# The routed blocks' early chains one unit sooner in the last step of a Mamba scan

## The chip, the cores and the metric

The program runs on one core of a Trainium2 chip. The metric is the device time in microseconds (us) of the whole program. Its engines each work through their own instructions in order and wait on semaphores: TensorE (PE: matrix products), VectorE (DVE), ScalarE (ACT), GpSimd (POOL), and SyncE (SP), which here only issues transfers.

## The reference

One transformer-like layer, float32, for 2 sequences of 2048 tokens with 256 features:

```python
h = _layernorm(x) * (1 + ca) + sa                      # modulated by a condition
x = x + ga * mixer(h)                                  # layernorm, then a Mamba forward and one backward in time
h = _layernorm(x) * (1 + cb) + sb
x = x + gb * ffn(h)

# in each Mamba (512 channels, 16 states), per time step:
h = h * exp(dt_t * A) + (dt_t * u_t) * B_t;  y = sum_n h * C_t
# out: (y + xc * D) * silu(z) @ W_out.T

# ffn: the best 2 of 8 experts by softmax of h @ gate_w.T, and a shared part for every token:
z = silu(xt @ sw1.T) * (xt @ sw2.T) @ sw3.T
```

## The kernel before

**Tiling.** The 4096 tokens are 8 blocks of 512. The mixer runs in 16 steps `q` (a block forward, a block backward, and so on). A step has 16 units `t`, each 32 channels by 16 states laid out as 128 partitions x 4 groups x 512 times; so there are 256 units `T = 16 q + t`. Four units are a chunk (128 channels).

**One unit.** ScalarE writes the four groups' decays `exp(dt * A)` into PSUM (`decay`, L1399, two at `n == 0` and two at `n == 2`), and at groups that start from a kept state adds it to the first input (`seed`, L1431). TensorE spreads a unit's 32 channels over the partitions (`spread_input`, L2480) into the one bank `PS_U`; VectorE multiplies it by B (`multiply`, L1914). For units 3, 7, 10, 12 and 15 of a step GpSimd does that multiply (L1046) from a copy that SyncE brings, except for unit 7 of the last step (`SPARED`). VectorE runs two scans (`scan`, L1935). GpSimd multiplies the result by C (`weigh`, L1058). When a chunk is complete TensorE sums it (`sum_chunk`, L2491 and L2495), and VectorE gates it (`gate_y`, L1900). `multiply(T + 1)` on VectorE stands ahead of `scan(T, 0)`, and waits for the `spread_input(T + 1)` that belongs to it.

**Order.** Nothing is scheduled by a program: each engine's order is the order in which its loop over `T` (on ScalarE: over `T` and `n` = 0 to 3) issues, and tables such as `Z_AT = [(5, 2), ...]` say at which `(t, n)` ScalarE does a side job. Within one `T`, TensorE's loop issues `spread_input`, then `sum_chunk`, and at its end `early_blocks(t)`. Two PSUM banks are shared in turn by everything that isn't scan work (`bank_uses`, `take_bank`, `filled`, `drained`): a product into a bank waits until the bank's last content has been copied out, which is ScalarE's work nearly always. The order of these uses is one list, and it is the same before and after.

**The last step (q = 15, units 240 to 255).** Two blocks of the feed-forward part are begun while the last scans run ("early blocks", p = 0 and 1): GpSimd adds the mixer's result (`weigh_mixed`, `add_mixed`); VectorE takes statistics (`norm_statistics`, L1970 and L1973); ScalarE copies them (`variance`); GpSimd takes the power (`norm_power`, L1105, `scale_mean`); ScalarE normalises (`normalise_tokens`, L1541); TensorE turns the block (`turn_early`, L2504), ScalarE copies it (`copy_turned_early`, L1524); TensorE makes the router's logits (`router_early`, L2515) and the shared part's products of block 0, four "g" (gate) and four "u", and four "g" of block 1 (`hidden_early`, L2535), each copied by ScalarE (`copy_g0`, `copy_u0`, `copy_g1`). In the same step ScalarE copies four z chunks (L1314) and takes silu of them at (7, 3), with a table load ahead of it and one behind. When the scans are over, VectorE, TensorE, ScalarE and GpSimd go through the eight blocks' feed-forward and routing by hand-written orders (from 1666 us on), and then through the tiles of the experts.

Of the kernel before, what the change touches and what calls it, by code (L numbers as in the profile page):

```python
# [29 lines left out]
STEPS = 2 * NBLK  # L30
# [42 lines left out]
OUT_AT = [(4, 1), (5, 0)]  # L73
Z_AT = [(5, 2), (6, 1), (6, 3), (7, 1)]

FIRST_Z_AT = [(5, 0), (5, 2), (6, 0), (6, 1)]
SILU_Z_AT = (7, 3)
XDBL_AT = (8, 0)
# [2 lines left out]
COPY_DT_AT = [(11, 1), (12, 2), (13, 3), (15, 2)]  # L81
XP0_AT, XP1_AT, CONV0_AT = (11, 3), (12, 3), (14, 1)

G0_AT = [(9, 3), (10, 1), (10, 3), (11, 1)]
U0_AT = [(12, 0), (12, 2), (12, 3), (12, 3)]
G1_AT = [(14, 1), (15, 1)]

EXP_AND_LN = "natural_log_exp_and_others"

# [113 lines left out]
def mixer_and_experts(nc, A, out):  # L203
    with ExitStack() as top:
# [760 lines left out]
        def _(pool):  # L965
# [153 lines left out]
            for T in range(ALL_UNITS):  # L1119
                q, t = divmod(T, UNITS)  # L1120
                ahead = q + 1 < STEPS
                if T + 2 < ALL_UNITS and on_pool(T + 2):
                    multiply(T + 2)
                if q == STEPS - 1 and t == 7:
                    add_mixed(1)
                if 0 < T < ALL_UNITS - 1:
                    weigh(T - 1)
                if t == 12 and ahead:
                    step_input(q + 1, 0)
                if T == 2:  # L1130
                    step_input(q, 2)
                if t == (6 if q > 0 else 9):
                    step_input(q, 3)
                if t == 14 and ahead:
                    step_input(q + 1, 1)
                if q == STEPS - 1:
                    if t == 2:
                        weigh_mixed(0)
                    if t == 3:
                        add_mixed(0)  # L1140
                        nc.gpsimd.memset(minus_half3[:], -0.5).then_inc(f_const, 1)
                    if t == 5:
                        pool.wait_ge(f_const, 1)
                        norm_power(0)
                        scale_mean(0)
                        weigh_mixed(1)
                    if t == 8:
                        norm_power(1)
                        scale_mean(1)
            def scatter(p, k):  # L1150
# [44 lines left out]
        def _(act):  # L1195
# [331 lines left out]
            def variance(p):  # L1527

                act.wait_ge(a_step, 2 * NT * (p + 1))
                nc.scalar.activation(fvar[:, p], fmv[:, p, :, 1], ACT.Copy, bias=EPS).then_inc(f_var, 1)  # L1530
                nc.scalar.activation(fmv[:, p, :, 0], fmv[:, p, :, 0], ACT.Copy, scale=-1.0).then_inc(f_var, 1)
# [67 lines left out]

            def early_blocks(t, n):  # L1600

                if (t, n) == (6, 0):
                    variance(0)
                if (t, n) == (6, 3):
                    normalise_tokens(0)
                if (t, n) in ((8, 0), (8, 1)):
                    copy_turned_early(0, n)
                if (t, n) == (9, 0):
                    copy_router(0)
                if (t, n) == (9, 2):  # L1610
                    variance(1)
                if (t, n) == (10, 3):
                    normalise_tokens(1)
                for c in range(NC):
                    if (t, n) == G0_AT[c]:
                        copy_g0(c)
                    if (t, n) == U0_AT[c]:
                        copy_u0(c)
                if (t, n) == (12, 1):
                    exp_scores(0)  # L1620
                if (t, n) == (13, 1):
                    copy_turned_early(1, 0)
                    copy_turned_early(1, 1)
                if (t, n) == (13, 3):
                    copy_router(1)
                if (t, n) in G1_AT:
                    copy_g1(G1_AT.index((t, n)))

            for T in range(ALL_UNITS):
                q, t = divmod(T, UNITS)  # L1630
                ahead = q + 1 < STEPS
                for n in range(NG):
# [27 lines left out]
                            back_to_exp()  # L1660
                    if q > 0 and (t, n) in OUT_AT:
                        copy_out(q - 1, OUT_AT.index((t, n)))
                    if (t, n) in (Z_AT if q > 0 else FIRST_Z_AT):
                        copy_z(q, (Z_AT if q > 0 else FIRST_Z_AT).index((t, n)))
                    if (t, n) == (XDBL_AT if q > 0 else FIRST_XDBL_AT) and ahead:
                        copy_x_dbl(q + 1)
                    if (T, n) == (6, 3):
# [188 lines left out]
        def _(dve):  # L1856
# [259 lines left out]

            def early_blocks(t):

                if t == 5:
                    norm_statistics(0)  # L2120
                if t == 8:
                    norm_statistics(1)
                if t == 11:
                    shift_logits(0)

            for D in range(2):
# [231 lines left out]
        def _(pe):  # L2358
# [179 lines left out]

            def early_blocks(t):

                if t == 7:
                    turn_early(0, 0)
                    turn_early(0, 1)
                if t == 8:
                    pe.wait_ge(f_gate_loaded, 48)
                    router_early(0)
                    pe.wait_ge(f_sw_loaded, 32)
                    hidden_early("g", 0, sw1, 0)
                    hidden_early("g", 0, sw1, 1)
                if t == 10:  # L2550
                    hidden_early("g", 0, sw1, 2)
                    turn_logits0()
                if t == 11:
                    hidden_early("g", 0, sw1, 3)
                    for c in range(NC):
                        hidden_early("u", 0, sw2, c)
                if t == 12:
                    turn_early(1, 0)
                    turn_early(1, 1)
                    router_early(1)  # L2560
                    hidden_early("g", 1, sw1, 0)
                if t == 14:
                    for c in range(1, NC):
                        hidden_early("g", 1, sw1, c)
                    turn_logits1()

            turn_block(0)
# [29 lines left out]
            for T in range(ALL_UNITS):  # L2597
# [27 lines left out]
                if T == 5:  # L2625
                    project_dt(0, 3)
                if T == SPARED - 2:
                    spread_input(T + 2)
                    project_z(q, 1)
                    project_z(q, 2)  # L2630
                if t % GN == 1 and T > GN:
                    sum_chunk(T // GN - 1)
# [391 lines left out]
```

## Time and profile before

| | us |
|---|---|
| three runs | 2057.31, 2058.60, 2059.46 |
| their median | 2058.6 |
| the profiled execution's own time | 2058.04 |
| its span | 2056.2 |
| busy: VectorE, TensorE, GpSimd, ScalarE | 1925.5, 1813.9, 1798.3, 1599.3 |
| units 240 to 255 on VectorE | about 1558 to 1665.7 |

A busy share over the whole program mixes three stages: the scans (to 1665.7 us), the blocks' feed-forward and routing (to about 1837 us), and the experts' tiles (to the end). The change touches only the last step of the first stage, so what counts is which engine has no idle time there and who waits for whom at the passage to the second stage.

### The profile page before, as it was taken

To read this page: it belongs to the slowest core of one execution; us is meant where nothing else is said; L and a number is where in the kernel's file an instruction comes from. 1 tells how busy PE (TensorE), PEld (TensorE's weight loads), DVE (VectorE), ACT (ScalarE), POOL (GpSimd) and SP (SyncE) were. 2 spreads that over 40 slices of the span, in tenths; PEclk is the share of its full clock that TensorE was granted. 3 is DMA by queue.
4 is the path that set the end of the run, shared out by engine and by line. 5 is a ranking of instruction groups with operands and counts; after the bars stand their busy time and mean duration, and the time that the engine had idled before them with its cause. 6 is when DMAs were issued, how large, how long until landed. Compare 5 with 4: busy or idle time off the path is not lost.

```text
span 2056.2 us, 25386 instructions
## 1 busy us (share of the span) xinstructions
PE 1813.9 (88%) x6768; PEld 829.7 (40%) x6768; DVE 1925.5 (94%) x1820; ACT 1599.3 (78%) x3362; POOL 1798.3 (87%) x612
## 2 busy tenths in 40 slices
PE   7788898979898979788898889898977799999997
PEld 3333333424242423232323233332322256569996
DVE  7999999999999999999999999999999998857776
ACT  5886779898989898877788898989896844546664
POOL 5689999999999999999999999999999953545555
PEclk9999898989898989898989989898987899999999
DMA  7736454544545353535362635354545334635555
GB/s 268 244 117 152 105 138 110 134 108 121 124 116 125 109 133 105 124 106 143 85 164 72 157 92 141 100 131 115 131 97 146 112 126 140 253 135 91 94 94 76
DMA packets 140653, 263.93 MB, mean 128 GB/s; under 512 B 21840, under 2 KB 44368, under 8 KB 139488
## 3 DMA queue, kind: packets, MB, share of 16 engines
q1 hardware_dynamic: 125920, 240.58, 43.3%
q0 software_dynamic: 13296, 17.80, 5.0%
q10 hardware_dynamic: 1296, 3.93, 0.5%
q8 instruction: 56, 0.92, 0.2%
q14 instruction: 85, 0.70, 0.1%
HBM read 193.10 MB, written 70.19 MB: 128 GB/s over the span
## 4 chain that ended last, share of the span: by engine, by line
PE 27%; ACT 23%; DVE 22%; issue 16%; POOL 11%; DMA 1%; DVEq 0%; ACTq 0%; POOLq 0%; SPq 0%
DVE hst L1935 13%; ACT psum L1399 9%; POOL hst L1058 7%; DVE dbu L1914 5%; PE psum L2739 4%; PE psum L2495 3%; PE psum L2925 3%; ACT dbu L1431 3%; PE psum L2934 3%; PE psum L2945 3%; PE psum L2753 2%; POOL dbu L1046 2%; PE psum L2415 2%; ACT sp_tmp L1368 1%; ACT dt L1363 1%
## 5 line engine op out<-in xcount | busy, mean ns | idle before, releaser
L1058 POOL TENSOR_TENSOR hst<-hst,c_rep 128x2048 f32<-128x2048 f32 x254 | 1146.8, 4548 | 3.5 <-ACT state L1385 3.4
L1399 ACT ACTIVATE psum<-dt_rep,neg_a 128x512 f32<-128x512 f32 (+1 forms) x1024 | 659.8, 676 | 123.1 <-DVE hst L1935 118.5
L1935 DVE TENSOR_TENSOR_SCAN hst<-psum,state,dbu 128x1024 f32<-128x1024 f32 x264 | 603.8, 2325 | 0.5 <-DVE score L2012 0.4
L1935 DVE TENSOR_TENSOR_SCAN hst<-psum,dbu 128x1024 f32<-128x1024 f32 x248 | 554.6, 2269 | 6.9 <-ACT psum L1399 6.8
L1914 DVE TENSOR_TENSOR dbu<-psum,b_rep 128x2048 f32<-128x2048 f32 x177 | 400.2, 2261 | 6.6 <-PE psum L2480 6.5
L1046 POOL TENSOR_TENSOR dbu<-dtu_rep,b_rep 128x2048 f32<-128x2048 f32 x79 | 360.1, 4559 | 12.4 <-DVE hst L1935 7.4
L2480 PE MATMUL psum<-dt,same 32*128 32x512 f32 x354 | 217.5, 696 | 103.0 <-DVE dbu L1914 94.9
L2495 PE MATMUL psum<-hst,same 128*32 128x512 f32 x2048 | 267.3, 669 | 43.2 <-POOL hst L1058 43.2
L2427 PE MATMUL psum<-xp,taps 128*128 128x512 f32 x512 | 237.1, 606 | 5.4 <-ACT sp_tmp L1365 5.3
L1189 POOL DMA_INDIRECT out_x<-h,target_u x71 | 110.8, 1560 | 107.1 <-issue 51.7
L1431 ACT ACTIVATE dbu<-first_decay,dbu,state 128x1 f32<-128x1 f32 x504 | 160.0, 376 | 20.5 <-DVE dbu L1914 18.9
L2495 PEld LDWEIGHTS psum<-hst,same 128*32 128x32 f32 x2048 | 65.5, 121 | 249.3 <-issue 159.5
L2427 PEld LDWEIGHTS psum<-xp,taps 128*128 128x128 f32 x512 | 95.5, 193 | 145.4 <-issue 145.4
L2480 PEld LDWEIGHTS psum<-dt,same 32*128 32x128 f32 x354 | 56.6, 197 | 215.2 <-DVE dbu L1914 134.5
L2408 PE MATMUL psum<-xnT,w_in 128*128 128x512 f32 x256 | 126.1, 626 | 14.0 <-ACT sp_tmp L1365 12.0
L2415 PE MATMUL psum<-xnT,w_in 128*128 128x512 f32 x256 | 122.7, 612 | 0.0
L2443 PE MATMUL psum<-w_out,sz 128*128 128x256 f32 x512 | 115.7, 379 | 0.0
L2461 PE MATMUL psum<-sp_tmp,w_dt 16*128 16x512 f32 x128 | 93.2, 842 | 20.0 <-ACT dt L1378 16.2
L2443 PEld LDWEIGHTS psum<-w_out,sz 128*128 128x128 f32 x512 | 97.3, 190 | 26.9 <-issue 15.3
L2491 PE MATMUL psum<-xc,diag_d 128*128 128x512 f32 x128 | 85.3, 754 | 16.9 <-DVE sz L1900 16.9
L1155 POOL DMA_INDIRECT slot_scratch<-send,slot_u x64 | 66.0, 1032 | 24.7 <-issue 17.7
L2739 PE MATMUL psum<-h2T,sw 128*128 128x512 f32 x192 | 87.2, 597 | 0.0
(246 smaller groups left out, 2623.9 us busy)
## 6 DMA issues: line engine op xcount, KB each, us to landing
dt_rep<-dt_scratch SPq DMA_DIRECT2D x256, 256.0 KB, 4.8
dtu_rep<-dtu_scratch SPq DMA_DIRECT2D x316, 64.0 KB, 1.9
taps<-taps_scratch SPq DMA_DIRECT2D x64, 256.0 KB, 4.5
b_rep<-bc_scratch SPq DMA_DIRECT2D x64, 256.0 KB, 4.9
c_rep<-bc_scratch SPq DMA_DIRECT2D x64, 256.0 KB, 7.7
dt_scratch<-dt SPq DMA_DIRECT2D x48, 256.0 KB, 6.2
h<-slot_scratch SPq DMA_DIRECT2D x71, 129.5 KB, 2.3
sp_tmp<-t_scratch SPq DMA_DIRECT2D x16, 512.0 KB, 6.9
```

The source lines that it names most:

```text
L1046: nc.gpsimd.tensor_tensor(dbu[:, U % DBU, :, :], dtu_rep[:].broadcast_to((P, NG, TB)), b_rep[U // UNITS % 2][:], ALU.mult).then_inc(pool_m ...
L1058: nc.gpsimd.tensor_tensor(h, h, c_rep[q % 2][:], ALU.mult).then_inc(prod_done, 1)
L1399: nc.scalar.activation(psum[:, PS_A + i, kept], dt_rep[:, G % 2, j, kept], ACT.Exp, scale=neg_a[:, q % 2, u, i:i + 1]).then_inc(exp_done, 1)
L1431: nc.scalar.activation(first, first_decay[:, u % GN, i:i + 1], ACT.Identity, scale=state[:, q % 2, u, i, :], bias=first).then_inc(seed_don ...
L1914: nc.vector.tensor_tensor(dbu[:, U % DBU, :, :], psum[:, PS_U:PS_U + 1, :].broadcast_to((P, NG, TB)), b_rep[U // UNITS % 2][:], ALU.mult). ...
L1935: nc.vector.tensor_tensor_scan(both(hst[:, U % RING, groups, :]), both(psum[:, PS_A + 2 * pair:PS_A + 2 * pair + 2, :]), both(dbu[:, U % D ...
L2415: ins = nc.tensor.matmul(psum[:, bank, :], w_in[:, q % 2, k, DI + c * P:DI + (c + 1) * P], xnT[:, q % 2, k, :], start=(k == 0), stop=(k == ...
L2427: ins = nc.tensor.matmul(psum[:, bank, :], taps[:, c % 2, j, :], xp[:, c % 2, at:at + TB], start=(j == 0), stop=(j == TAPS - 1))
L2443: ins = nc.tensor.matmul(psum[:, bank, half * DM:(half + 1) * DM], sz[:, c, tok], w_out[:, q % 2, c, :], start=False, stop=(half == 1 and ...
L2480: nc.tensor.matmul(psum[:, PS_U, :], same[part, :], dtu[part, c, :], start=True, stop=True).then_inc(u_full, 1)
L2495: ins = nc.tensor.matmul(psum[CH * j:CH * (j + 1), PS_Y, :], same[:, 0:CH], hst[:, (GN * G + j) % RING, i, :], start=False, stop=(i == NG ...
L2739: ins = nc.tensor.matmul(psum[:, bank, :], w[:, k, c * P:(c + 1) * P], h2T[:, j % 2, k, :], start=(k == 0), stop=(k == KD - 1))
```

## The change

In the last step, the early blocks' jobs move to earlier places in the loops; no instruction is added or removed, and no size changes.

- GpSimd: `weigh_mixed(0)` at t = 1 (was 2), `add_mixed(0)` at 2 (was 3) and ahead of that unit's `weigh`, `norm_power`, `scale_mean` and `weigh_mixed(1)` at 4 (was 5), `add_mixed(1)` at 6 (was 7), `norm_power(1)` at 7 (was 8).
- VectorE: statistics at t = 4 and 7 (were 5 and 8), `shift_logits(0)` at 10 (was 11).
- ScalarE: own places for the last step's z copies; both `variance`, `normalise_tokens`, `copy_turned_early` and `copy_router`, and the copies of g and u, up to six places sooner.
- TensorE: `early_blocks` begins at t = 6 (was 7), the first block's third g product stands ahead of the sum of chunk 61, the u products at t = 10 (were 11), the second block at t = 11 (was 12), and `project_z(q, 1)` ahead of a `spread_input`.

```diff
+LAST_Z_AT = [(5, 2), (5, 3), (6, 1), (7, 0)]
-G0_AT = [(9, 3), (10, 1), (10, 3), (11, 1)]
-U0_AT = [(12, 0), (12, 2), (12, 3), (12, 3)]
-G1_AT = [(14, 1), (15, 1)]
+G0_AT = [(8, 3), (9, 1), (9, 3), (11, 0)]
+U0_AT = [(11, 1), (11, 2), (11, 3), (12, 0)]
+G1_AT = [(13, 2), (15, 1)]
...  GpSimd
-                if q == STEPS - 1 and t == 7:
+                if q == STEPS - 1 and t == 2:
+                    add_mixed(0)
+                if q == STEPS - 1 and t == 6:
                     add_mixed(1)
...
-                    if t == 8:
+                    if t == 7:
                         norm_power(1)
                         scale_mean(1)
...  ScalarE, early_blocks(t, n)
-                if (t, n) in ((8, 0), (8, 1)):
+                if (t, n) in ((7, 0), (7, 1)):
                     copy_turned_early(0, n)
-                if (t, n) == (9, 0):
+                if (t, n) == (8, 0):
+                    variance(1)
                     copy_router(0)
-                if (t, n) == (9, 2):
-                    variance(1)
-                if (t, n) == (10, 3):
+                if (t, n) == (9, 3):
                     normalise_tokens(1)
...
-                if (t, n) == (13, 1):
+                if (t, n) == (12, 2):
                     copy_turned_early(1, 0)
                     copy_turned_early(1, 1)
...  VectorE
-                if t == 8:
+                if t == 7:
                     norm_statistics(1)
...  TensorE, early_blocks(t)
-                if t == 10:
+                if t == 8:
                     hidden_early("g", 0, sw1, 2)
                     turn_logits0()
-                if t == 11:
+                if t == 9:
                     hidden_early("g", 0, sw1, 3)
+                if t == 10:
                     for c in range(NC):
                         hidden_early("u", 0, sw2, c)
-                if t == 12:
+                if t == 11:
                     turn_early(1, 0)
                     turn_early(1, 1)
                     router_early(1)
                     hidden_early("g", 1, sw1, 0)
...
                 if T == SPARED - 2:
+                    project_z(q, 1)
                     spread_input(T + 2)
-                    project_z(q, 1)
                     project_z(q, 2)
```

On TensorE, units 248 to 253, before. `dt,same` is a `spread_input` (in the order shown: of units 251, 253, 254), `hst,same` a chunk's sum (61, then 62), `x1,sw1` a g product of block 0, `x1,sw2` its u products, `dt_rep,sw1` the first g product of block 1; two matmuls are one product.

```order
L2480 MATMUL psum<-dt,same 128x512
L2515 MATMUL psum<-x1,gate 32x128 x8
L2535 MATMUL psum<-x1,sw1 128x512 x4
L2491 MATMUL psum<-xc,diag_d 128x512
L2495 MATMUL psum<-hst,same 32x512 x16
L2535 MATMUL psum<-x1,sw1 128x512 x2
L2523 MATMUL psum<-ident,turned_logits 128x128
L2480 MATMUL psum<-dt,same 128x512
L2535 MATMUL psum<-x1,sw1 128x512 x2
L2535 MATMUL psum<-x1,sw2 128x512 x8
L2480 MATMUL psum<-dt,same 128x512
L2504 MATMUL psum<-ident,tin 128x128 x8
```

The same place after the change (from the router of block 0 on; `dt,same` is unit 251, then 253, then 254):

```order
L2516 MATMUL psum<-x1,gate 32x128 x8
L2536 MATMUL psum<-x1,sw1 128x512 x4
L2481 MATMUL psum<-dt,same 128x512
L2536 MATMUL psum<-x1,sw1 128x512 x2
L2524 MATMUL psum<-ident,turned_logits 128x128
L2492 MATMUL psum<-xc,diag_d 128x512
L2496 MATMUL psum<-hst,same 32x512 x16
L2536 MATMUL psum<-x1,sw1 128x512 x2
L2536 MATMUL psum<-x1,sw2 128x512 x8
L2481 MATMUL psum<-dt,same 128x512
L2505 MATMUL psum<-ident,tin 128x128 x8
L2516 MATMUL psum<-dt_rep,gate 32x128 x8
```

The `spread_input` of unit 253 stood ahead of the fourth g and the four u products and now stands behind them; that of unit 254, which stood ahead of the turning of block 1 (`ident,tin`), now stands behind that, block 1's router and its first g product.

## Rows read from the trace of the kernel before

**Rows 1.** The page, part 1: busy us (share of the span) xinstructions.

```profile
PE 1813.9 (88%) x6768; PEld 829.7 (40%) x6768; DVE 1925.5 (94%) x1820; ACT 1599.3 (78%) x3362; POOL 1798.3 (87%) x612
```

**Rows 2.** Windows: stretch, length, each engine's busy us (instructions), TensorE's granted clock, DMA.

```profile
1666.00:1680.00 14.00, 14.00 (x55) 10.07 (x54) 13.86 (x29) 5.94 (x6) 6.72 (x21) 1.00 0.18 61
1720.00:1770.00 50.00, 50.00 (x214) 29.76 (x216) 43.50 (x142) 24.83 (x56) 27.58 (x28) 1.00 0.73 271
```

**Rows 3.** Timeline of VectorE, last step: start us, us, line, operation [idle before].

```profile
1620.64 4.59 DVE L1935 TENSOR_TENSOR_SCAN hst<-psum,state,dbu 128x1024 f32<-128x1024 f32 x2
...
1637.65 2.35 DVE L1935 TENSOR_TENSOR_SCAN hst<-psum,state,dbu 128x1024 f32<-128x1024 f32 x1 [0.35 <-DVE score L2012]
...
1642.76 2.27 DVE L1914 TENSOR_TENSOR dbu<-psum,b_rep 128x2048 f32<-128x2048 f32 x1
...
1649.44 2.27 DVE L1914 TENSOR_TENSOR dbu<-psum,b_rep 128x2048 f32<-128x2048 f32 x1
...
1660.60 2.27 DVE L1935 TENSOR_TENSOR_SCAN hst<-psum,dbu 128x1024 f32<-128x1024 f32 x1
...
1690.48 0.69 DVE L1900 TENSOR_TENSOR sz<-psum,sz 128x512 f32<-128x512 f32 x1 [1.16 <-PE psum L2495]
```

**Rows 4.** Timeline of ScalarE, last step.

```profile
1608.99 0.84 ACT L1420 ACTIVATE first_decay<-neg_a,dt_rep 128x4 f32<-128x4 f32 x4
1611.73 0.60 ACT L1314 ACTIVATE sz<-psum 128x512 f32<-128x512 f32 x1 [1.89 <-PE psum L2415]
...
1613.53 1.28 ACT L1324 ACT_TABLE_LOAD   x1
...
1618.62 1.28 ACT L1399 ACTIVATE psum<-dt_rep,neg_a 128x511 f32<-128x511 f32 x2
1619.84 1.43 ACT L1524 ACTIVATE x<-psum,mod_turned 128x512 f32<-128x512 f32 x2
```

**Rows 5.** Timeline of GpSimd, last step.

```profile
1619.77 4.56 POOL L1046 TENSOR_TENSOR dbu<-dtu_rep,b_rep 128x2048 f32<-128x2048 f32 x1
1624.25 4.56 POOL L1058 TENSOR_TENSOR hst<-hst,c_rep 128x2048 f32<-128x2048 f32 x1
1628.74 1.05 POOL L1105 TENSOR_TENSOR frstd<-fvar,minus_half 128x4 f32<-128x4 f32 x1
```

**Rows 6.** Timeline of TensorE; four L2535 entries are one product.

```profile
1572.09 5.07 PE L2495 MATMUL psum<-hst,same 128*32 128x512 f32 x32 [2.41 <-POOL hst L1058]
...
1628.86 3.64 PE L2495 MATMUL psum<-hst,same 128*32 128x512 f32 x32
...
1634.46 1.12 PE L2480 MATMUL psum<-dt,same 32*128 32x512 f32 x2
1635.51 5.60 PE L2535 MATMUL psum<-x,sw 128*128 128x512 f32 x12
...
1644.74 1.98 PE L2535 MATMUL psum<-x,sw 128*128 128x512 f32 x4 [0.76 <-ACT x L1567]
1646.66 1.12 PE L2480 MATMUL psum<-dt,same 32*128 32x512 f32 x2
...
1650.62 1.08 PE L2515 MATMUL psum<-dt_rep,gate 128*32 128x128 f32 x16 [1.82 <-ACT dt_rep L1524]
1651.64 2.90 PE L2535 MATMUL psum<-dt_rep,sw 128*128 128x512 f32 x4
...
1664.26 7.03 PE L2773 MATMUL psum<-dt_rep,sw 128*128 128x512 f32 x16
```

**Rows 7.** Windows of 2 us around the sum at 1572 us, as in rows 2.

```profile
1572.00:1574.00 2.00, 1.92 (x12) 0.60 (x16) 2.00 (x2) 0.67 (x2) 2.00 (x2) 0.50 0.12 45
1574.00:1576.00 2.00, 2.00 (x20) 0.44 (x12) 2.00 (x2) 1.30 (x2) 2.00 (x1) 0.75 0.00 0
```

**Rows 8.** SyncE's loads of sw1 and sw2, and the landing of all three sw loads.

```profile
1611.72 0.83 SPq L811 DMA_DIRECT2D sw<-in_sw  x2
...
DMA to landing us min/median/max: 3.9/6.0/6.5
```

More of the change, by code:

```diff
@@ L1136, in _ @@
                 if q == STEPS - 1:
-                    if t == 2:
+                    if t == 1:
                         weigh_mixed(0)
-                    if t == 3:
-                        add_mixed(0)
                         nc.gpsimd.memset(minus_half3[:], -0.5).then_inc(f_const, 1)
-                    if t == 5:
+                    if t == 4:
                         pool.wait_ge(f_const, 1)
@@ L1600, in early_blocks @@
             def early_blocks(t, n):
+                if (t, n) == (5, 0):
+                    variance(0)
                 if (t, n) == (6, 0):
-                    variance(0)
-                if (t, n) == (6, 3):
                     normalise_tokens(0)
-                if (t, n) in ((8, 0), (8, 1)):
+                if (t, n) in ((7, 0), (7, 1)):
                     copy_turned_early(0, n)
-                if (t, n) == (9, 0):
+                if (t, n) == (8, 0):
+                    variance(1)
                     copy_router(0)
-                if (t, n) == (9, 2):
-                    variance(1)
-                if (t, n) == (10, 3):
+                if (t, n) == (9, 3):
                     normalise_tokens(1)
@@ L1620, in early_blocks @@
                     exp_scores(0)
-                if (t, n) == (13, 1):
+                if (t, n) == (12, 2):
                     copy_turned_early(1, 0)
                     copy_turned_early(1, 1)
-                if (t, n) == (13, 3):
+                if (t, n) == (13, 0):
                     copy_router(1)
@@ L1662, in _ @@
                         copy_out(q - 1, OUT_AT.index((t, n)))
-                    if (t, n) in (Z_AT if q > 0 else FIRST_Z_AT):
-                        copy_z(q, (Z_AT if q > 0 else FIRST_Z_AT).index((t, n)))
+                    z_at = FIRST_Z_AT if q == 0 else Z_AT if ahead else LAST_Z_AT
+                    if (t, n) in z_at:
+                        copy_z(q, z_at.index((t, n)))
                     if (t, n) == (XDBL_AT if q > 0 else FIRST_XDBL_AT) and ahead:
@@ L2117, in early_blocks @@
             def early_blocks(t):
-                if t == 5:
+                if t == 4:
                     norm_statistics(0)
-                if t == 8:
+                if t == 7:
                     norm_statistics(1)
-                if t == 11:
+                if t == 10:
                     shift_logits(0)
@@ L2539, in early_blocks @@
             def early_blocks(t):
-                if t == 7:
+                if t == 6:
                     turn_early(0, 0)
                     turn_early(0, 1)
-                if t == 8:
+                if t == 7:
                     pe.wait_ge(f_gate_loaded, 48)
@@ L2549, in early_blocks @@
                     hidden_early("g", 0, sw1, 1)
-                if t == 10:
+                if t == 8:
                     hidden_early("g", 0, sw1, 2)
                     turn_logits0()
-                if t == 11:
+                if t == 9:
                     hidden_early("g", 0, sw1, 3)
+                if t == 10:
                     for c in range(NC):
                         hidden_early("u", 0, sw2, c)
-                if t == 12:
+                if t == 11:
                     turn_early(1, 0)
@@ L2561, in early_blocks @@
                     hidden_early("g", 1, sw1, 0)
-                if t == 14:
+                if t == 13:
                     for c in range(1, NC):
                         hidden_early("g", 1, sw1, c)
+                if t == 14:
                     turn_logits1()
```

## The prediction

> **What bounds the kernel now.** I read the busy shares first. VectorE has 94% of the span and GpSimd 87% [rows 1], but those are means over stages, so I went on to the stage that the change touches. In VectorE's timeline of the last step the reader is to see that each instruction begins where the one before ends; the only idle time is 0.35 us at 1637.65 [rows 3]. So VectorE bounds the last step. Nothing that makes another engine earlier can shorten it by more than that, while whatever makes VectorE wait lengthens it in full. Then the passage to the next stage. TensorE begins the second block's u products at 1664.26 [rows 6] and from there on has no idle time: 14.00 of 14 us and, later, 50.00 of 50 [rows 2]. Those products need the last unit's first scan, which ended at 1660.60 + 2.27 = 1662.87 [rows 3]. So TensorE is late by 1664.26 - 1662.87 = 1.4 us there, and a delay of VectorE costs the program its size less 1.4 us. VectorE has a little slack later too (1.16 us idle at 1690.48 [rows 3]), so that a delay is passed on through TensorE and not twice.
>
> **The change, part by part.** No instruction is added, so each engine's work is the same and only waits can differ. I go along the chain in which a moved job meets a tight place. "Wanted" is the time at which VectorE comes to an instruction in the trace of before.
>
> *Statistics, variance, normalising, turning of block 0.* VectorE's 1.9 us of statistics only change places with other VectorE work. Their inputs are ready: GpSimd's reordered jobs are the same jobs. I cost these at nothing; VectorE's and GpSimd's own unbroken work hides them.
>
> *The z copies and silu (term A).* The last z copy ran when TensorE delivered, at 1611.73; ScalarE was idle 1.89 us before it, having already done the first decays (0.84 us) [rows 4]. With one `spread_input` behind a z product instead of ahead, and copies that fall a little sooner, I take the last z as 0.4 us earlier (an estimate; 0 to 0.7 by the idle time it could come out of). But now two turned copies (1.43 us) stand between this z copy and silu, and the first decays (0.84 us) stand behind the copy too [rows 4]. Behind silu and its two table loads (they begin at 1613.53) stand the decays of unit 248, which ended at 1618.62 + 1.28 = 1619.90 [rows 4]. They now end at 1619.9 - 0.4 + 1.43 + 0.84 = 1621.8. VectorE's scan of unit 248 began at 1620.64 [rows 3] and now waits: 1.1 us (0.5 to 1.5).
>
> *GpSimd's power (term B, no delay of its own).* `norm_power(1)` came after the `weigh` of unit 247 and now stands ahead of GpSimd's multiply of unit 250. It needs `variance(1)`, which ScalarE does behind those same decays, at 1622.0. GpSimd arrives at 1619.77 [rows 5] and waits 2.2 us, with the multiply and the `weigh` of 247 queued behind. That `weigh` ended at 1624.25 + 4.56 = 1628.81; it now ends 2.2 us (wait) + 1.4 us (the power's 1.05 us [rows 5] and an estimated 0.35 for the scaling behind it) later, at 1632.4.
>
> *The fourth g and the u products, ahead of the `spread_input` of unit 253 (term C).* TensorE is in order: the sum of chunk 61 waits for that `weigh`, then come one g product, four u products, and only then the `spread_input` that VectorE's multiply of unit 253 needs. In the trace it ran at 1634.46, more than 8 us ahead of the multiply at 1642.76 [rows 3, 6]: this cover is gone. The sum took 3.64 us at the full clock, and 5.07 us where TensorE had waited for GpSimd with nothing to do and the granted clock stood at 0.50 (1.2 GHz) until past 1574 [rows 6, 7]. In the new order TensorE has done its g product, the logits and the diagonal product by about 1629 and waits some 3 us for the `weigh`, so I take the nearer row, 5.07 us: to 1637.5. Five products at 5.60 / 3 = 1.87 us [rows 6] make 9.3 us: to 1646.8. The `spread_input` takes 1.12 us: 1647.9. ScalarE's copies, which free the two banks in between, are 0.6 us each and fit beside the products. So the multiply of unit 253 runs at 1647.9 instead of 1642.76: VectorE is 5.1 us late in all, A included. With the sum at 3.64 us it is 3.7 us.
>
> *Block 1 ahead of the `spread_input` of unit 254 (term D).* VectorE wants it 1649.44 - 1642.76 = 6.7 us after the multiply of 253 [rows 3], now at 1654.6. In between, ScalarE must copy the last u product, do decays and the two turned copies (to about 1650.5), then TensorE does the router and the g product, which ran from 1650.62 to 1651.64 + 2.90 = 1654.54 [rows 6], 3.9 us, and the 1.12 us of the `spread_input`: 1655.6. That is 1.0 us more (0 to 2.0).
>
> *The rest.* The sw loads issue when the last z product is done, as before, and land up to 6.5 us later [rows 8], near 1618; the first g product may wait for that, but the second waits for ScalarE's router copy at about 1622 anyway. The decay rows of the last chunk and GpSimd's inputs are fetched by SyncE after GpSimd's multiply of unit 250, so about 3.6 us later; ScalarE needs them only after the delayed fourth g copy, so they are covered, and if not ScalarE's first decays wait for them (in the third rival). `shift_logits` one unit sooner keeps its 0.35 us. The copies of g1 a place sooner free a bank early, for nothing: the last still falls in unit 255.
>
> **The sum.** VectorE is late by 5.1 + 1.0 = 6.1 us (A 1.1, C 4.0, D 1.0). Of it 1.4 us is TensorE's lateness at 1664.26. That leaves +4.7 us; I take 4.5, since the hand-over 0.4 to 0.7 us earlier could be the larger of the two. The profiled execution took 2058.04 us, a span of 2056.2 and 1.8 around it; it would take 2062.5. It lies 0.6 us under the median of the three runs, so for the median: 2058.6 + 4.5 = 2063.1 us.
>
> **A rule beside the rows.** In rows 6 the `spread_input` of 254 at 1646.66 begins only when the u product ahead of it (1644.74 + 1.98), which itself had waited 0.76 us for ScalarE, is over. The Trainium skill says the same (PSUM — Partial Sum Buffer, section Engine vs sequencer instructions): a weight load may run ahead of matmuls under way, but matmuls start and complete in program order. If they didn't, term C would vanish, and the first rival's time would hold.
>
> **Rivals.**
> 1. *Not slower.* The `spread_input`s are in time after all: the mechanism is that early work leaves TensorE free before the last scan. TensorE would start the last u products at 1662.87, 1.4 us earlier: 2058.6 - 1.4 = 2057.2 us. For it speaks that TensorE's lateness is real. Against it, five products and a sum behind a `weigh` that ended at 1628.81 even in the old order give 1628.8 + 3.6 + 9.3 + 1.1 = 1642.8, exactly when VectorE wants the multiply; the point from which it decides is that GpSimd isn't held. I give it 8%.
> 2. *The full clock.* The gap ahead of the sum is short or the clock has just risen, so the sum takes 3.64 us: VectorE 3.7 us late. The second `spread_input` then adds nothing (0 of term D), so +2.3: 2060.9 us. 25%.
> 3. *More serial than I count.* TensorE stays at the low clock through several of the u products (one g product took 2.90 us [rows 6]; three of five at that cost 3.1 us more) or the decay rows come late: +7.6: 2066.2 us. 12%.
> 4. *My forecast*, 55%, with a range of its own of 2061.9 to 2064.3.
>
> **Chances.** A measurement of this kernel can tell about 0.2% from no change, 4.1 us, that is up to 2062.7 us. Of the forecast's 55% I put 34 above it and 21 below. Slower by over 0.2%: 34 + 12 = 0.46. Within: 21 + 25 + 6 of the first rival = 0.52. Faster: 0.02, since even that rival gives only 1.4 us. For 8 times in 10 the range leaves out most of the first rival and the far part of the third: 2059.0 to 2066.0.
>
> **What would show it.** In the changed profile VectorE's timeline should have idle time at three places of the last step: about 1.1 us ahead of the scans of unit 248, released by ScalarE; 2 to 4 us ahead of the multiply of unit 253 and part of it perhaps at the second scan of unit 251 (decays behind the u copies), released by TensorE L2481; up to 2 us ahead of the multiply of 254. GpSimd should wait about 2 us for `variance(1)` ahead of `norm_power(1)`. The last scan should end near 1671.7 instead of 1665.6, and the last u products should start 4 to 5 us later. I am wrong if VectorE has no idle time there, if TensorE's `spread_input` of 253 runs ahead of 1642.7, or if the stage behind 1666 us gives back more than 1.4 us.

## The result: 0.26% slower

| | us |
|---|---|
| before, 7 runs | 2057.45 median (2057.21 to 2059.46) |
| after, 7 runs | 2063.65 median (2061.51 to 2067.39) |
| ratio after to before | 1.0026, 95% interval 1.0017 to 1.0036 |
| the profiled execution of after | 2066.62, its span 2064.8 |

The forecast was 2063.1 us with a range of 2059.0 to 2066.0. The ratio of 1.0026 is 5.4 us of 2058 (3.5 to 7.4); the two medians lie 6.2 us apart, within the same interval. The seven times of after stand in two groups, four from 2061.51 to 2063.65 and three from 2066.62 to 2067.39, and the profile is of the upper group.

Line numbers of after are one higher than those of before in VectorE's and ScalarE's code (multiply L1915, scan L1936, decays L1400), and L2481, L2496, L2536 and L2776 on TensorE for the `spread_input`, a chunk's sum, the early products and the last u products. First VectorE's timeline of the last step (start us, us, operation, [idle before it and what ended it]), which answers to [rows 3]:

```profile
1579.85 0.66 DVE L1901 TENSOR_TENSOR sz<-psum,sz 128x512 f32<-128x512 f32 x1
...
1612.52 2.29 DVE L1915 TENSOR_TENSOR dbu<-psum,b_rep 128x2048 f32<-128x2048 f32 x1 [1.24 <-PE psum L2481]
...
1624.85 4.59 DVE L1936 TENSOR_TENSOR_SCAN hst<-psum,state,dbu 128x1024 f32<-128x1024 f32 x2 [1.45 <-ACT psum L1400]
...
1637.38 6.83 DVE L1936 TENSOR_TENSOR_SCAN hst<-psum,state,dbu 128x1024 f32<-128x1024 f32 x3 [0.35 <-DVE score L2013]
...
1648.89 2.29 DVE L1915 TENSOR_TENSOR dbu<-psum,b_rep 128x2048 f32<-128x2048 f32 x1 [1.83 <-PE psum L2481]
...
1658.63 2.29 DVE L1915 TENSOR_TENSOR dbu<-psum,b_rep 128x2048 f32<-128x2048 f32 x1 [2.96 <-PE psum L2481]
...
1669.83 2.26 DVE L1936 TENSOR_TENSOR_SCAN hst<-psum,dbu 128x1024 f32<-128x1024 f32 x1
...
1698.68 0.69 DVE L1901 TENSOR_TENSOR sz<-psum,sz 128x512 f32<-128x512 f32 x1 [0.18 <-PE psum L2496]
```

The first row is VectorE's gate in unit 242. The same row of before is:

```profile
1578.66 0.65 DVE L1900 TENSOR_TENSOR sz<-psum,sz 128x512 f32<-128x512 f32 x1
```

From this gate on both traces can be laid over each other; after's times are 1.19 us later there. (The kernel before, profiled again as r10, had the gate at 1578.05, and r8, another kernel that changes nothing ahead of it, had it at 1580.31, so these 1.2 us need not be the change's.) I call the *stretch* the time from this gate to the start of the last u products: 1664.26 - 1578.66 = 85.60 us before, 1672.23 - 1579.85 = 92.38 us after, 6.78 more. What is left of the 8.6 us between the two spans is the 1.19 us ahead of the gate and 0.63 us behind the u products. Four waits of VectorE where before had none (the 0.35 is old) sum to 1.24 + 1.45 + 1.83 + 2.96 = 7.48 us. VectorE's instructions themselves take 0.54 us more from the gate to the end of unit 255's first scan (84.11 us busy against 83.57). TensorE's lateness behind VectorE gave back 1.25 us: the first scan of unit 255 ends at 1669.83 + 2.26 = 1672.09 and the u products start 0.14 us behind it, where it was 1.39 us.

TensorE's timeline says who made VectorE wait. It answers to [rows 6]:

```profile
1597.52 3.78 PE L2416 MATMUL psum<-xnT,w_in 128*128 128x512 f32 x4 [4.03 <-ACT sp_tmp L1319]
1601.23 2.07 PE L2481 MATMUL psum<-dt,same 32*128 32x512 f32 x2
1603.23 3.77 PE L2416 MATMUL psum<-xnT,w_in 128*128 128x512 f32 x4
...
1607.79 3.64 PE L2496 MATMUL psum<-hst,same 128*32 128x512 f32 x32
1611.36 1.12 PE L2481 MATMUL psum<-dt,same 32*128 32x512 f32 x2
1612.41 1.98 PE L2416 MATMUL psum<-xnT,w_in 128*128 128x512 f32 x4
...
1625.16 3.78 PE L2536 MATMUL psum<-x,sw 128*128 128x512 f32 x4 [4.12 <-ACT turned_logits L1553]
1628.87 2.07 PE L2481 MATMUL psum<-dt,same 32*128 32x512 f32 x2
1630.88 3.60 PE L2536 MATMUL psum<-x,sw 128*128 128x512 f32 x4
...
1635.38 3.64 PE L2496 MATMUL psum<-hst,same 128*32 128x512 f32 x32
1638.95 8.85 PE L2536 MATMUL psum<-x,sw 128*128 128x512 f32 x20
1647.73 1.12 PE L2481 MATMUL psum<-dt,same 32*128 32x512 f32 x2
...
1651.80 1.08 PE L2516 MATMUL psum<-dt_rep,gate 128*32 128x128 f32 x16 [1.93 <-ACT dt_rep L1525]
1652.81 3.78 PE L2536 MATMUL psum<-dt_rep,sw 128*128 128x512 f32 x4
1656.53 2.07 PE L2481 MATMUL psum<-dt,same 32*128 32x512 f32 x2
```

Three times TensorE waits for ScalarE (4.03, 4.12 and 1.93 us), and behind each wait the same product takes 3.8 us instead of 1.98, the same `spread_input` 2.07 instead of 1.12. Each time the next `spread_input` that VectorE needs stands behind it: that of unit 248 (1611.36), 253 (1647.73), 254 (1656.53). The windows give the reason (stretch, length, TensorE's busy us, granted clock, DMA share, GB/s):

```profile
1598.00:1602.00 4.00, 4.00 (x5) 0.50 0.49 163
1602.00:1606.00 4.00, 4.00 (x6) 0.50 0.19 50
1606.00:1610.00 4.00, 4.00 (x28) 0.89 0.00 0
...
1626.00:1630.00 4.00, 4.00 (x6) 0.50 0.00 0
1630.00:1634.00 4.00, 4.00 (x6) 0.50 0.35 75
1634.00:1650.00 16.00, 15.87 (x66) 0.99 0.73 216
...
1654.00:1658.00 4.00, 4.00 (x6) 0.50 0.00 0
```

At 0.50 (1.2 GHz) TensorE is 4.00 of 4 us busy and gets through 5 or 6 instructions. So the first and the third wait cost twice, once themselves and once in slow products. The slow products behind the second cost nothing of their own: the sum behind them needs GpSimd's `weigh(247)`, which ended near 1635.3, and it began at 1635.38.

The low clock at the first of these places is not new. These are lines of before, from the timelines of VectorE, ScalarE and TensorE: the statistics of block 0, the out copy (the copy of the output projection's result, L1318), `spread_input(247)` and the two z products:

```profile
1596.80 1.38 DVE L1970 BATCH_NORM_STATS2 fstats<-x 128x6 f32<-128x256 f32 x4
...
1593.78 0.57 ACT L1318 ACTIVATE sp_tmp<-psum 128x512 f32<-128x512 f32 x1
...
1596.92 2.07 PE L2480 MATMUL psum<-dt,same 32*128 32x512 f32 x2 [4.64 <-DVE dbu L1914]
...
1598.92 5.37 PE L2415 MATMUL psum<-xnT,w_in 128*128 128x512 f32 x8
```

And the first two of them in after:

```profile
1591.44 1.39 DVE L1971 BATCH_NORM_STATS2 fstats<-x 128x6 f32<-128x256 f32 x4
...
1596.89 0.57 ACT L1319 ACTIVATE sp_tmp<-psum 128x512 f32<-128x512 f32 x1
```

Before, the `spread_input` stood ahead of both z products, and the two took 5.37 us together, without a wait of VectorE. In after VectorE's statistics (1.9 us) come one unit sooner, so the scans behind them run later. The out copy stands behind decays that wait for those scans, and it comes 1.92 us later (1596.89 - 1.19 = 1595.70 against 1593.78). The z product waits for this out copy, and the `spread_input` for the z product.

GpSimd's `norm_power(1)` waited 3.75 us where it had waited for nothing in [rows 5]:

```profile
1624.93 1.02 POOL L1106 TENSOR_TENSOR frstd<-fvar,minus_half 128x4 f32<-128x4 f32 x1 [3.75 <-ACT fvar L1531]
...
1630.75 9.05 POOL L1059 TENSOR_TENSOR hst<-hst,c_rep 128x2048 f32<-128x2048 f32 x2
```

The first of the two instructions in the last line is `weigh(247)`.

### The profile page after: what moved, and what is told of

Read it like the earlier page. It is cut to its first block and busy times, and to the rows that moved or that the text cites. A ratio compares the mean times of both kernels' runs of the same rounds, so it can differ in the third digit from the quotient of the medians.

```text
span 2064.8 us, 25386 instructions
## 1 busy us (share of the span) xinstructions
PE 1817.4 (88%) x6768; PEld 829.1 (40%) x6768; DVE 1925.2 (93%) x1820; ACT 1598.1 (77%) x3362; POOL 1796.6 (87%) x612
## 5 line engine op out<-in xcount | busy, mean ns | idle before, releaser
L1400 ACT ACTIVATE psum<-dt_rep,neg_a 128x512 f32<-128x512 f32 (+1 forms) x1024 | 659.8, 676 | 122.8 <-DVE hst L1936 116.8
L1936 DVE TENSOR_TENSOR_SCAN hst<-psum,state,dbu 128x1024 f32<-128x1024 f32 x264 | 604.5, 2330 | 1.9 <-ACT psum L1400 1.5
L1936 DVE TENSOR_TENSOR_SCAN hst<-psum,dbu 128x1024 f32<-128x1024 f32 x248 | 554.9, 2271 | 10.5 <-ACT psum L1400 9.3
L1915 DVE TENSOR_TENSOR dbu<-psum,b_rep 128x2048 f32<-128x2048 f32 x177 | 400.8, 2264 | 11.1 <-PE psum L2481 10.9
L2496 PE MATMUL psum<-hst,same 128*32 128x512 f32 x2048 | 267.8, 670 | 44.8 <-POOL hst L1059 44.8
L2481 PE MATMUL psum<-dt,same 32*128 32x512 f32 x354 | 217.3, 695 | 93.5 <-DVE dbu L1915 83.3
L2496 PEld LDWEIGHTS psum<-hst,same 128*32 128x32 f32 x2048 | 65.4, 121 | 253.1 <-issue 160.8
L2481 PEld LDWEIGHTS psum<-dt,same 32*128 32x128 f32 x354 | 56.5, 197 | 207.8 <-DVE dbu L1915 122.3
```

What stands on the lines that cost most here:

```text
L1400: nc.scalar.activation(psum[:, PS_A + i, kept], dt_rep[:, G % 2, j, kept], ACT.Exp, scale=neg_a[:, q % 2, u, i:i + 1]).then_inc(exp_done, 1)
L1915: nc.vector.tensor_tensor(dbu[:, U % DBU, :, :], psum[:, PS_U:PS_U + 1, :].broadcast_to((P, NG, TB)), b_rep[U // UNITS % 2][:], ALU.mult). ...
L1936: nc.vector.tensor_tensor_scan(both(hst[:, U % RING, groups, :]), both(psum[:, PS_A + 2 * pair:PS_A + 2 * pair + 2, :]), both(dbu[:, U % D ...
L2481: nc.tensor.matmul(psum[:, PS_U, :], same[part, :], dtu[part, c, :], start=True, stop=True).then_inc(u_full, 1)
L2496: ins = nc.tensor.matmul(psum[CH * j:CH * (j + 1), PS_Y, :], same[:, 0:CH], hst[:, (GN * G + j) % RING, i, :], start=False, stop=(i == NG ...
```

## The experiments

Times are medians. r1 to r4, and r9 and r10, ran on chips where the kernel before took 2072 to 2073 us, r5 to r8 where it took 2059.55, so each is told as a ratio to before on its own chip. All ten carry one more edit, GpSimd's wait for `counts[s] & 1023` instead of `counts[s]`, which is the same number; r10 is before with it, r1 is after with it. "Waits" are VectorE's in the stretch, from its timeline, with the engine that ended them, without the old 0.35. The stretch and the waits are those of one profiled execution each; the ratio comes from all timed ones.

| | ratio to before (95% interval) | stretch us | waits us |
|---|---|---|---|
| before | | 85.60 | none |
| after | 1.0026 (1.0017 to 1.0036) | 92.38 | 1.24 PE, 1.45 ACT, 1.83 PE, 2.96 PE |
| r10 before again | 1.0001 (0.9991 to 1.0012) | 85.75 | none |
| r1 after again | 1.0040 (1.0026 to 1.0054) | 91.42 | 1.30 PE, 1.45 ACT, 1.87 PE, 1.12 PE |
| r2 spread 253 first | 1.0037 (1.0023 to 1.0050) | 91.17 | 1.24 PE, 1.46 ACT, 1.08 ACT, 1.79 PE |
| r3 block 1 later | 1.0031 (1.0020 to 1.0042) | 91.35 | 1.32 PE, 1.45 ACT, 1.88 PE, 0.94 ACT |
| r4 both | 1.0015 (1.0005 to 1.0025) | 91.70 | 1.35 PE, 1.45 ACT, 3.66 ACT |
| r5 z order back | 1.0030 (1.0018 to 1.0041) | 90.46 | 1.66, 1.29, 0.98 ACT, 1.78 PE |
| r6 clock kept up | 1.0009 (1.0000 to 1.0018) | 87.15 | 0.28 ACT, 1.90 PE |
| r7 turned copies behind silu | 1.0039 (1.0024 to 1.0053) | 92.79 | 1.32 PE, 2.12, 1.64 ACT, 1.09, 1.43 PE |
| r8 before, copies sooner | 1.0003 (0.9994 to 1.0012) | 84.41 | none |
| r9, r6 and r4 together | 0.9998 (0.9987 to 1.0008) | 87.94 | 3.26 ACT |

**r10, before again.** No edit.

> The kernel before as it is. Every theory expects the same time as before, within 0.1 per cent; it shows what a stretch from the gate of unit 242 to the last u products, and the time, differ by from one execution and one chip to another: 85.6 us plus or minus 0.3 if the waits are set by the order alone; more if the granted clock changes the waits of this kernel too.

The stretch was 85.75 us, 0.15 from before's, although the whole program took 2072 us in this execution and 2058 in before's.

**r1, after again.** No edit.

> The changed kernel once more, with one register operation on GpSimd in the experts' tiles (the count that its scatter waits for is masked with 1023), as in all runs that follow. Both theories: 2061 to 2067 us, 4 to 10 us over the kernel before, and VectorE idle ahead of the scans of unit 248 and the multiplies of units 253 and 254. If the spread of the times (2061.5 to 2067.4 so far) comes from TensorE's granted clock in the last step, this profile shows waits of another size at the same places.

Three waits came back within 0.06 us. The fourth, ahead of the multiply of 254, was 1.12 us instead of 2.96: one and the same order waits differently there from one execution to the next. The timed ratio of 1.0040 is 8.3 us of 2072 (5.4 to 11.2), more than the 5.8 us that this profile's stretch is longer; where the rest lies wasn't shown.

**r2, the `spread_input` of 253 ahead of the u products.** It then stands behind the sum of chunk 61 and the fourth g product.

```diff
-                if T + 2 < ALL_UNITS and T not in (6, SPARED - 2) ...:
+                if T + 2 < ALL_UNITS and T not in (6, SPARED - 2, ALL_UNITS - 5) ...:
                     spread_input(T + 2)
+                if T == ALL_UNITS - 6:
+                    spread_input(T + 3)
```

> Only the spread_input of unit 253 goes back ahead of the u products. Theory 1 (one chain): the multiply of 254 still waits for the same chain through the u products and block 1, so its wait grows by what the wait of 253 (1.8 us) loses; VectorE's last scan ends at the same time, time within 0.5 us of the changed kernel. Theory 2 (separate waits that add up, as the prediction summed them): the time falls by 1.8 us or more.

The wait ahead of the multiply of 253 went, and 1.08 us for ScalarE's decays and 1.79 us at 254 stood in its place. The stretch gained 0.25 us on r1's, so the waits are not separate costs that add up.

**r3, block 1's turn, router and first g product back.**

```diff
-                if t == 11:
+                if t == 12:
                     turn_early(1, 0)
```

> Only block 1's turning, router and first g product on TensorE go back to t = 12, behind the spread_input of unit 254. Theory 1 (one chain): the wait ahead of the multiply of 254 (3.0 us) goes; the waits at 248 and 253 stay; time 2.5 to 3 us under the changed kernel, less what TensorE is then late by at the last u products. Theory 2: the same 3 us. A rival by which the g products behind the last scans decide: no gain, since block 1 ends later.

The wait for TensorE ahead of the multiply of 254 went, and 0.94 us for ScalarE's decays took its place: no gain in the stretch against r1 (0.07 us), where 2.5 to 3 us were expected.

**r4, the edits of r2 and r3 together.**

> Both edits of the two runs before together. Theory 1: the waits at 253 and 254 are both gone, 4.8 us less for VectorE's last scan, more than the two single gains together (0 + 3); what stays is the wait of the scans of 248 and of the multiply of 248, about 2.7 us, of which 1.4 us were free before; time 4 to 5 us under the changed kernel and 1 to 3 us over the kernel before. Theory 2: the gain is the sum of the two single gains.

No wait for a `spread_input` was left behind unit 248, and the stretch was still 91.70 us. But the profiled execution is the slowest of nine (2078.57 us, 2.5 above their median), and the interval of the ratio ends at 1.0025 where r1's begins at 1.0026: timed, the two edits together gave back 3.7 us by the medians and 5.2 by the ratios, and this profile doesn't show where. What follows holds for this execution. Three rows of TensorE's timeline, then VectorE's wait:

```profile
1626.74 1.98 PE L2536 MATMUL psum<-x,sw 128*128 128x512 f32 x4
...
1633.94 6.49 PE L2496 MATMUL psum<-hst,same 128*32 128x512 f32 x32 [4.12 <-POOL hst L1059]
1640.36 1.98 PE L2536 MATMUL psum<-x,sw 128*128 128x512 f32 x4
```

```profile
1647.29 2.35 DVE L1936 TENSOR_TENSOR_SCAN hst<-psum,state,dbu 128x1024 f32<-128x1024 f32 x1 [3.66 <-ACT psum L1400]
```

The g products ran at the full clock this time, but then TensorE waited 4.12 us for GpSimd's `weigh(247)`, and the sum took 6.49 us. ScalarE copies the fourth g ahead of the decays of unit 251, so VectorE waited for ScalarE instead. Here one wait covers another: the sum ends late with or without the `spread_input`s behind it. That the g products were fast and the sum slow isn't the edits' doing, for it begins ahead of both: the first g product waited 2.41 us for its load (1.10 in r2) and took 3.64 us, and the second then waited 1.07 us instead of 4.04.

**r5, `spread_input(247)` ahead of the z product again.**

```diff
-                    project_z(q, 1)
                     spread_input(T + 2)
+                    project_z(q, 1)
                     project_z(q, 2)
```

> The changed kernel with only the spread_input of unit 247 back ahead of the z product. Theory 1 (one chain that begins at the last z copy and runs through silu, the router copy, the g and u products and block 1): the wait of the multiply of 248 (1.24 us) goes, the z products end up to 1.3 us sooner, and all that hangs on them too; from the fourth-last gate_y (unit 242) to the last u products about 90 to 91 us instead of 91.4 to 92.4; before 85.6. Theory 2 (separate waits): only the 1.24 us go. The two differ in the wait ahead of the scans of unit 248: smaller by theory 1, 1.45 us as before by theory 2.

The 1.24 us went, but TensorE now had nothing to do for longer:

```profile
1599.18 2.07 PE L2481 MATMUL psum<-dt,same 32*128 32x512 f32 x2 [6.54 <-DVE dbu L1915]
1601.18 6.18 PE L2416 MATMUL psum<-xnT,w_in 128*128 128x512 f32 x8
```

The two z products take 6.18 us together where full speed takes 2 x 1.98. ScalarE copies their results ahead of decays, and VectorE waited 1.66 and 1.29 us for those. TensorE's order is before's here, and its wait is 1.90 us longer than before's 4.64: as much as VectorE's statistics, which stand ahead of the multiply that it waits for. No run put them back alone, so what they cost by themselves stays open. The stretch gained 1.0 us of the 5.8 that r1 has more than before.

**r6, the clock kept up.** Four matmuls are added while TensorE would wait for the out copy; they write a bank that is free and nobody reads the result.

```diff
+                    pe.wait_ge(yg_done, GN * 15)
+                    for _ in range(4):
+                        nc.tensor.matmul(psum[:, PS_Y, :], diag_d[:, q % 2, 0, :], xc[:, q % 2, 0, :],
+                                         start=True, stop=True)
                     project_z(q, 1)
```

> The changed kernel with four extra matmuls (chunk 60's bank, overwritten later) ahead of the second z product, in the gap of 4 us in which TensorE waits for ScalarE; it adds work and no wait. If the granted clock is what makes the z products late (3.78 + 2.07 + 3.77 us at the low clock), they take 1.98 + 1.12 + 1.98 us, the wait of the multiply of 248 goes, silu and all behind it come 2 to 4 us sooner: 89 to 90 us from unit 242's gate to the last u products. If the order alone matters, nothing changes, or it costs up to 1 us.

```profile
1592.67 3.70 PE L2633 MATMUL psum<-xc,diag_d 128*128 128x512 f32 x8
1596.77 1.98 PE L2416 MATMUL psum<-xnT,w_in 128*128 128x512 f32 x4 [0.40 <-ACT sp_tmp L1319]
1599.28 1.12 PE L2481 MATMUL psum<-dt,same 32*128 32x512 f32 x2 [0.53 <-DVE dbu L1915]
1600.33 1.98 PE L2416 MATMUL psum<-xnT,w_in 128*128 128x512 f32 x4
...
1630.77 4.93 PE L2496 MATMUL psum<-hst,same 128*32 128x512 f32 x32 [3.33 <-POOL hst L1059]
1635.62 8.85 PE L2536 MATMUL psum<-x,sw 128*128 128x512 f32 x20
1644.40 1.12 PE L2481 MATMUL psum<-dt,same 32*128 32x512 f32 x2
```

```profile
1594.00:1598.00 4.00, 3.60 (x9) 1.00 0.10 40
1598.00:1602.00 4.00, 3.47 (x8) 1.00 0.45 150
```

The granted clock stood at 1.00 where it had been 0.50, the z products took 1.98 us, and the waits of 1.24 and 1.45 us and the one at 254 were gone. More work on TensorE made the stretch 4.3 us shorter than in r1 and 5.2 shorter than in after, and shorter than the 89 to 90 us expected. The wait at 253 stayed: 1.90 us, behind a sum that TensorE reached early (3.33 us idle), took 4.93 us for, and five products. That is the mechanism of the forecast almost alone, and its price: 87.15 - 85.60 = 1.55 us of stretch, ratio 1.0009.

**r7, block 0's turned copies behind silu.**

```diff
-                if (t, n) in ((7, 0), (7, 1)):
-                    copy_turned_early(0, n)
                 if (t, n) == (8, 0):
                     variance(1)
+                    copy_turned_early(0, 0)
+                    copy_turned_early(0, 1)
                     copy_router(0)
```

> The changed kernel with block 0's two turned copies behind silu and the decays of unit 248, at (8, 0). Theory 1 (one chain): VectorE's 1.45 us ahead of the scans of 248 goes, but the router copy, which waits for these copies, comes about 1 us later, so the waits at 253 and 254 grow by what was gained: 91 to 93 us from unit 242's gate to the last u products. Theory 2 (separate waits): 1.4 us less, 90 to 91 us.

```profile
1625.86 1.08 PE L2516 MATMUL psum<-x,gate 128*32 128x128 f32 x16 [8.31 <-ACT x L1525]
```

TensorE's router waited 8.31 us for the turned copies. The wait of 1.45 us ahead of unit 248's first scan went, so the turned copies did hold up those decays, as term A says; but 2.12 us ahead of its second scan and 1.64 us ahead of unit 249's, both for decays, took its place. The turned copies are work of ScalarE that has to be done somewhere between a late z copy and the late decays.

**r8, the kernel before with only its last copies sooner.**

```diff
-U0_AT = [(12, 0), (12, 2), (12, 3), (12, 3)]
-G1_AT = [(14, 1), (15, 1)]
+U0_AT = [(11, 3), (12, 0), (12, 2), (12, 3)]
+G1_AT = [(13, 3), (15, 1)]
...  block 1's turned copies at (12, 3), its router copy at (13, 1)
```

> The kernel before, with only ScalarE's copies of the u products, of block 1's turning and router and of its first g product sooner (u at (11, 3), (12, 0), (12, 2), (12, 3), turning at (12, 3), router at (13, 1), g at (13, 3)); every spread_input stays ahead. By theory 1 TensorE gets ahead without making VectorE wait: the last u products start when the last unit's first scan is done, up to 1.4 us sooner than before (84.2 to 85.6 us from unit 242's gate), time 0 to 1.4 us under the kernel before. A rival: a copy placed sooner makes ScalarE wait for TensorE ahead of decays, VectorE waits, and it is 1 us slower.

```profile
1664.72 7.11 PE L2773 MATMUL psum<-dt_rep,sw 128*128 128x512 f32 x16 [0.48 <-DVE hst L1935]
```

TensorE now waits for VectorE there, the stretch is 1.19 us shorter than before's, and VectorE has no new wait. That is the useful part of the change, without its price. In the timed runs it isn't shown: the ratio of 1.0003 cannot tell 1.2 us (0.06%) from nothing.

**r9, the edits of r6, r2 and r3 together.** As in r2 the `spread_input` of 253 stands behind the sum and the fourth g product, not ahead of the sum as the expectation has it.

> The changed kernel with two edits together: the four added matmuls ahead of project_z(q, 1) that kept the granted clock up (their result isn't used), and the two moves of r4 (spread_input(253) issued ahead of the sum of chunk 61 and of the u products; block 1's turn, router and g_0 back behind t = 12, so that spread_input(254) isn't behind them). Theory (two causes that add: a fallen clock that makes the z, g and u products late, and spreads that stand behind those products): with the clock up only the 1.90 us wait of the multiply of 253 was left on VectorE (and 0.28 ahead of it), and this takes its spread out from behind the products, so VectorE has no wait over 0.5 us but shift_logits' 0.35; from the gate of unit 242 to the start of the last u products 85.3 to 86.0 us (before: 85.60; clock alone: 87.15), time within 0.1 per cent of before. Rival (the chain of blocks itself is late: ScalarE takes the u copies ahead of the decays when the products end early, as in r4, where the wait turned into 3.66 us on ScalarE's decays): a wait of 1.5 to 3 us for ScalarE stands in its place, the stretch stays at 87 us or more, and the ratio stays about 1.001.

```profile
1629.95 6.60 PE L2496 MATMUL psum<-hst,same 128*32 128x512 f32 x32 [3.39 <-POOL hst L1059]
1636.48 1.98 PE L2536 MATMUL psum<-x,sw 128*128 128x512 f32 x4
```

```profile
1643.42 2.35 DVE L1936 TENSOR_TENSOR_SCAN hst<-psum,state,dbu 128x1024 f32<-128x1024 f32 x1 [3.26 <-ACT psum L1400]
```

The rival held in the trace: one wait of 3.26 us for ScalarE's decays, which stand behind the copy of the fourth g, which stands behind a sum of 6.60 us. The time is no different from before's (0.9998), but the profiled stretch is 87.94 us, no better than r6. The comparison flatters r6: up to this sum both have the same order, and it took 4.93 us in one execution and 6.60 in the other, 1.67 us that are no edit's. Against r10, on the same chip, r9's stretch is 2.2 us longer and its span only 0.5, for behind the start of the u products it took 404.44 us and r10 406.30. Why it took less there, and whether other executions waited less, stays open.

## Why the prediction was right, and where its steps were off

The starting point held: VectorE had no slack, so every wait showed in the end, and 1.25 of the 1.4 us of TensorE's lateness came back. The time fell into the range in good part by luck, as the sum at the end says. With after's times put back by 1.19 us, step by step:

- **Term A (1.1 us predicted ahead of the scans of 248, for ScalarE): 1.45 us.** Right in place and size, partly for the wrong reason. I took the last z copy as 0.4 us *earlier*; it ran at 1614.43, put back 1613.24, 1.5 us *later* than in [rows 4], since the z products ahead of it ran at the low clock. VectorE being late itself by 1.24 us hid most of it. r6 has no wait there: its z copy ran 30.65 us behind the gate, where before's ran 33.07 behind it, and then the added jobs cost VectorE nothing.
- **The failed step: the last step's z products, taken as unhindered.** The prediction took the last z copy as 0.4 us earlier for one `spread_input` behind a z product, and put the move of VectorE's statistics at nothing. In its place the runs showed a z product that waits 4.03 us for ScalarE's out copy (1.92 us later than before, behind the moved statistics), `spread_input(247)` queued behind it, and both z products at 0.50, 3.78 and 3.77 us. That made the 1.24 us ahead of the multiply of 248, which no step foresaw. The place of the `spread_input` is the small part: in r5 that wait is gone, waits for ScalarE stand in its place, and 1.0 us of stretch came back. The low clock is the large part: with it up (r6) the waits of 1.24 and 1.45 us and that at 254 were gone, and 4.3 to 5.2 us of the stretch.
- **Term B (2.2 us of GpSimd): 3.75 us.** The same row ahead, bigger by as much as ScalarE was later. The sum of chunk 61 started at 1634.2, put back, instead of 1632.4.
- **Term C (multiply of 253 at 1647.9, VectorE 5.1 us late with A): 1648.89 - 1.19 = 1647.70, 4.9 us late.** The total is right by errors that cancel: the sum started 1.8 us later than predicted, took 1.4 us less, and the products 0.5 us less. The sum took 3.64 us at the full clock and not 5.07, for TensorE didn't idle ahead of it: it arrived with slow g products (3.78 and 3.60 us) just as `weigh(247)` ended. The five products took 8.85 us (9.3 predicted). In r6 the picture of the prediction does hold: idle 3.33 us, a sum of 4.93 us. The order as mechanism is shown by r2: with the `spread_input` out from behind the products the wait for it was gone. But the gain was 0.25 us, since ScalarE's decays, behind the copies of the same products, were late as well. The rule beside the rows was borne out: a `spread_input` behind products began when the last of them ended, to within 0.1 us (in after 1638.95 + 8.85 = 1647.80 and 1647.73).
- **Term D (1.0 us, up to 2.0): 2.96 us in the profile, 1.12 in r1.** The router started at 1650.61 (1650.5 predicted), but its g product took 3.78 us instead of 2.90 and the `spread_input` 2.07 instead of 1.12, both at 0.50. This 1.8 us that one execution has and another hasn't is the mis-sized part of this term, and its cause is the third rival's, a clock that stays low, at another product. Whether the two groups of after's times come from it alone wasn't shown; r1's stretch was 1.0 us shorter.

Sum: 4.7 us forecast for the stretch, 5.8 (r1) and 6.8 (after) measured, 5.4 (3.5 to 7.4) in the timed ratio. That these lie so near is luck in good part. The forecast's own chain, with the clock up at the z products, cost 1.55 us of stretch (r6), a third of what was forecast; the low clock there, for which the sum has no term, made up the rest and more. The u products were to start 4 to 5 us later, and VectorE to be 6.1 us late; it was 6.8 and, at the end of unit 255's first scan, 92.24 - 84.21 = 8.0 us. The first rival is out: TensorE does reach the last products with VectorE, as it said, but VectorE comes 7.5 us of waits later. The second rival, the full clock with a small second wait, had the sum's 3.64 us right and nothing else.

## What to carry to other kernels

Before an in-order engine's instruction is moved behind another, ask what that other one waits for: the cover of the moved one must hold the wait, and on TensorE also the slower clock behind the wait, which doubled products here (1.98 to 3.78 us). When each of several edits, undone alone, gives back at most 1.0 us of stretch (r2, r3, r5) and one that touches no order gives back four (r6), the waits are likely one chain, and its head is the place to mend. Which that is, a comparison of both kernels' rows ahead of the first wait tells: here an out copy 1.9 us later, behind work that had been moved "at no cost". Starting a chain sooner is worth no more than the idle time at its end: 1.2 us here in r8's profile, against 5.4 paid on the bounding engine.

## What the runs showed of the chip

- The same 32 matmuls of a chunk's sum took 3.64 us at the full clock, 4.93 us behind 3.33 us of idle time (r6), and 6.49 and 6.60 us behind 4.12 and 3.39 us (r4, r9). The idle time ahead of it does not tell the price; the granted clock while it runs does: in r6 it was 0.65 from 1632 to 1634 us and 1.00 behind that, in r9, whose sum began 0.8 us sooner, 0.50 until 1634 and 0.51 until 1636.
- After the 4.03 us of idle time that ended at 1597.52 the granted clock stayed at 0.50 from 1598 to 1606 us, with TensorE busy throughout, so a wait can slow work well behind it. It need not: behind the same 1.93 us of wait the first g product of block 1 took 3.78 us in after, 2.89 in r1 and 1.98 in r5 and r6.
- Whole programs differed by 13 us between chips (before: 2059.55 and 2072.95 us) while the stretch of before, without idle time on VectorE, differed by 0.15 us; in the profiles the difference lies behind the scans (391.94 us from the last u products on in before, 406.30 in r10).
